# A graph-layer kernel's edge sort: four-record chunks, batches of 28 columns in two groups, the last bucket's true end, and one logit moved

## The chip, the cores and the metric

The kernel runs on one core of one Trainium2 chip. The metric is device time in microseconds; lower is better. Names of engines: PE is TensorE, DVE is VectorE, ACT is ScalarE, POOL is GpSimd, SP is SyncE, which only issues transfers and waits.

## What is computed

```python
xn = _layernorm(x)                                   # x: 6250 nodes x 256
x = x + gnn(xn, edge_weight, edge_weight_n2, ..., src, dst) + mix(xn)
x = x + ffn(_layernorm(x))                           # the best half of the nodes, by a score
...
# gnn: 106250 edges
low  = relu(segment_sum(val_low[:, None]  * (xn @ weight_low)[col],  row))    # row = src, col = dst
high = relu(segment_sum(val_high[:, None] * (xn @ weight_high)[col], row))
mlp  = relu(xn @ weight_mlp)
logits = concat([low @ att_low, high @ att_high, mlp @ att_mlp])
att = softmax(sigmoid(logits) @ att_vec / 3)
out = 3 * (att[:, 0:1] * low + att[:, 1:2] * high + att[:, 2:3] * mlp)
```

`mix` is an attention with one 32 x 32 matrix per head, summed over all nodes, and a GELU layer behind it.

## The kernel before, in words

The edges come unordered by `src`. The kernel sorts them into 98 buckets of 64 nodes, and then sums each bucket with matmuls.

**The sort.** The edges lie on 128 partitions. A batch is BB = 30 columns of them (3840 edges), and there are G = 28 batches. A batch is split into GROUPS = 3 groups of GS = 10 columns. For each batch DVE builds one-hots (`one_hot`, L733), sums them (`sum_hots`, L746 to L752), PE adds them up into ranks (`ranks`), ACT copies the ranks (`copy_rank`, L1313), DVE picks each edge's rank (`pick_rank`, L766) and makes its place (`place`, L777 to L793). ACT turns the places into one-hots, group by group (`quotients`: one activation per column, L1303, then one ReLU over the group, L1307), DVE multiplies records with cells (`cell_records`, L811), and PE permutes the batch with one matmul per column (`permute`). `stage_records` (L1322) copies the result; `destinations` (L827, L829) makes the indices; POOL scatters it to `sorted_records` in DRAM (`scatter`, L648) with UNITS = 16 indirect DMAs, each of which writes for 128 partitions one chunk of two records (32 bytes). Each batch's share of a bucket is padded to a whole number of chunks.

**What goes on beside it.** `schedule` puts one batch in a slot, and gives the first 14 slots the layer norm (`ln_moments`, `ln_apply`) and the attention's K and V sums for 13 quads of node tiles, and the later slots the rest of `mix` (`hidden`, `mlp`, `mix_end`, `mix_out`). Slot 13 folds the weights. With SPILL = 2 the last two mixes run in slots after the last batch. `mix_out` also makes the third attention logit, a product and a sum over a quad (L895, L898, into `l3`). Each engine runs its list in the order that its `slot` writes. In a mix slot PE permutes groups 0 and 1 of the batch before, transposes the first pair of tiles (`turn(0)`, L1602), permutes group 2, transposes the second pair, and goes on to destinations, the mix and the next ranks. ACT begins a slot with the quotients of group 2 of the batch before, right behind `copy_rank`.

**The bucket loop.** SP loads the sorted records; PE and ACT turn them to columns of 128 records. POOL gathers, column by column, the 128 rows of `xn_rows` that a column's records name, into a ring of 32 columns (L665). SP counts what has landed (`g_ready`, in fours) and tells POOL which columns are free (`col_free`, L564). Two buckets are one tile of 128 nodes. For each bucket DVE makes the weighted one-hots (`select`, L1116 and L1122), PE multiplies them with ten columns from the bucket's first on (five, then five), and with one more in a loop for each column beyond ten (`extras`). ACT copies the sums (L1490 and L1443), then come the two weight matmuls, the attention, and the FFN for the tile, spread over three stages. `ptab` holds where each bucket begins. Its entries from 98 on are set to the table's end, `COLS * P - 1`, so the last bucket reaches to column 851.

**The tail** picks the best half of the nodes by a search over thresholds, and stores the result.

```python
COLS = 4 * -(-(E + NB * G) // (4 * P))                          # 852 columns
for u in range(UNITS):                                          # scatter, L646
    pool.indirect_dma_start(rec_dram, ..., stage_rec[0:PR, par, u * 8:(u + 1) * 8], None)
for j in range(GS):                                             # quotients, L1302
    ins = act.activation(quot[:, j, :], iota32[:, :], ACT.Abs, ...)
act.activation(flat, flat, ACT.Relu, bias=ones_f[:, 0:1], scale=-1.0)
step(dve.memset(pclip[:, NB:NR], float(COLS * P - 1)))          # the last bucket's end
```

## Time and profile before

| | us |
|---|---|
| median of 3 timed runs | 1985.35 (1983.74 to 1985.68) |
| profiled execution, first to last instruction | 2481.7 |
| its time as a run of its own | not recorded beside the span |
| busy in it: PE, DVE, ACT, POOL | 1719.4, 1229.1, 924.8, 1371.7 |

The profiled execution is 496 us longer than the timed ones. Its span is told in microseconds from the first instruction. The sort runs from 63 us (the first scatter) to 813 us, the bucket loop from 832 to 2405 us, the tail to 2481.7 us. A matmul of PE in fp32 leaves two records; ends of matmuls are modelled. "issue" marks idle time for which the profile shows no wait.

### The profile page before, as it was taken

The numbers are of one execution on the slowest core, as the hardware profiler recorded it, in microseconds if no ns is written. First come the engines' busy times: TensorE is split into PE (matmuls) and PEld (weight loads), VectorE is DVE, ScalarE is ACT, GpSimd is POOL, SyncE is SP. The second block draws the span as 40 slices with busy tenths as digits, with TensorE's granted clock in tenths as the row PEclk, the third lists the DMA queues.
The fourth block names the chain that finished last, engine by engine and source line by source line (L and its number), as shares of the span: only waits on it lengthen the run. The fifth ranks groups of instructions, "written<-read, shape, count | busy, mean of one in ns | idle before, by whom it ended". The sixth has DMA issues, their size and how long they took to land.

```text
span 2481.7 us, 30518 instructions
## 1 busy us (share of the span) xinstructions
PE 1719.4 (69%) x9109; PEld 1441.9 (58%) x9109; DVE 1229.1 (50%) x3164; ACT 924.8 (37%) x2641; POOL 1371.7 (55%) x1351
## 2 busy tenths in 40 slices
PE   4788884998865347776777677677577677667672
PEld 4566673887754335665665666566466566556562
DVE  8899995888761223432343333333333333333336
ACT  2677873777652112321222222222222222222223
POOL 3277675788776565545555455455455545554600
PEclk9899996999967667888887888788788788788886
DMA  3221211111100422222222222222222222222303
GB/s 90 72 63 54 80 33 30 46 54 46 46 5 5 133 85 72 78 69 75 71 74 71 68 73 75 65 72 75 68 73 75 75 69 71 81 71 68 85 9 104
DMA packets 102212, 162.99 MB, mean 66 GB/s; under 512 B 32190, under 2 KB 72762, under 8 KB 102040
## 3 DMA queue, kind: packets, MB, share of 16 engines
q0 software_dynamic: 55232, 113.59, 16.4%
q1 hardware_dynamic: 46808, 47.29, 6.0%
q8 instruction: 85, 1.39, 0.2%
q14 instruction: 87, 0.71, 0.1%
HBM read 139.76 MB, written 21.04 MB: 65 GB/s over the span
## 4 chain that ended last, share of the span: by engine, by line
PE 51%; issue 23%; DVE 10%; ACT 9%; another core or an unknown queue 5%; DMA 1%; SPq 1%; POOL 0%; DVEq 0%; ACTq 0%; POOLq 0%
PE bank L1528 49%; ACT side L1303 2%; PE bank L1817 1%; ACT base L1303 1%; ACT arena L1303 1%; DVE arena L811 1%; ACT arena L1447 1%; ACT arena L1443 1%; DVE arena L733 1%; ACT side L1519 1%; DVE arena L766 1%; ACT arena L1307 0%; PE bank L1602 0%; DVE arena L781 0%
## 5 line engine op out<-in xcount | busy, mean ns | idle before, releaser
L1528 PE MATMUL bank<-arena 128*128 128x128 f32 (+3 forms) x6320 | 1292.5, 359 | 508.2 <-issue 426.8
L1528 PEld LDWEIGHTS bank<-arena 128*128 128x128 f32 (+1 forms) x6320 | 1094.8, 205 | 683.8 <-issue 500.0
L665 POOL DMA_INDIRECT arena<-xn_rows,arena x852 | 825.5, 969 | 733.8 <-SPq L564 450.0
L648 POOL DMA_INDIRECT sorted_records<-arena x448 | 523.0, 1167 | 256.0 <-issue 139.3
L1167 DVE CUSTOM_DVE_ANT_0 arena<-arena 128x256 f32<-128x256 f32 x98 | 37.8, 423 | 414.9 <-ACT arena L1452 376.1
L1122 DVE TENSOR_TENSOR arena<-arena 128x640 f32<-128x640 bf16 (+1 forms) x204 | 164.2, 805 | 47.6 <-DVE arena L1116 17.7
L1172 DVE SCALAR_TENSOR_TENSOR att_prod<-sg,att_neg 128x9 f32<-128x9 f32 x49 | 8.5, 174 | 334.9 <-issue 300.8
L1490 ACT ACTIVATE arena<-bank 128x256 f32<-128x256 f32 x49 | 18.8, 383 | 355.5 <-remote 262.1
L1116 DVE SCALAR_TENSOR_TENSOR arena<-io,arena 128x320 bf16<-128x320 f32 (+1 forms) x204 | 97.8, 479 | 106.3 <-DVE wall L1209 43.5
L1528 PE MATMUL bank<-arena,base 128*128 128x128 f32 (+3 forms) x766 | 118.4, 287 | 16.7 <-ACT base L1307 8.3
L1438 ACT ACTIVATE arena<-bank,b1f 128x128 f32<-128x128 f32 x392 | 110.3, 372 | 33.5 <-PE bank L1528 28.1
L811 DVE TENSOR_TENSOR arena<-arena 128x1280 f32<-128x1280 bf16 x84 | 120.5, 1488 | 4.1 <-remote 1.7
L1528 PEld LDWEIGHTS bank<-arena,base 128*128 128x128 f32 (+2 forms) x766 | 110.2, 211 | 17.6 <-ACT base L1307 8.5
L1443 ACT ACTIVATE arena<-bank 128x256 f32<-128x256 f32 x49 | 18.8, 383 | 247.0 <-PE bank L1528 219.3
L1528 PE MATMUL bank<-side,arena 128*128 128x512 f32 x196 | 97.1, 619 | 0.3 <-issue 0.3
L1481 ACT ACTIVATE side<-bank,wall 128x256 f32<-128x256 f32 x49 | 23.1, 472 | 176.0 <-remote 165.3
L1303 ACT ACTIVATE base<-arena 128x128 f32<-128x128 f32 x280 | 84.7, 391 | 9.4 <-DVE arena L792 9.4
L1468 ACT ACTIVATE nr<-nri 128x1 f32<-128x1 f32 x49 | 9.9, 203 | 206.0 <-issue 159.8
L1303 ACT ACTIVATE arena<-arena 128x128 f32<-128x128 f32 x280 | 84.6, 397 | 0.0
L1303 ACT ACTIVATE side<-arena 128x128 f32<-128x128 f32 x280 | 84.6, 392 | 0.0
L1528 PE MATMUL bank<-arena,side 128*128 128x128 f32 x560 | 73.5, 282 | 12.0 <-issue 10.9
L1528 PEld LDWEIGHTS bank<-arena,side 128*128 128x128 f32 x560 | 68.0, 196 | 15.6 <-issue 14.1
(312 smaller groups left out, 1889.2 us busy)
## 6 DMA issues: line engine op xcount, KB each, us to landing
arena<-xn_rows,arena POOLq DMA_INDIRECT x852
sorted_records<-arena POOLq DMA_INDIRECT x448
arena<-in_x SPq DMA_DIRECT2D x12, 512.0 KB
xn_rows<-arena SPq DMA_DIRECT2D x12, 512.0 KB
x_plus_xn_rows<-arena SPq DMA_DIRECT2D x12, 512.0 KB
arena<-x_plus_xn_rows SPq DMA_DIRECT2D x12, 512.0 KB
arena<-xn_rows SPq DMA_DIRECT2D x12, 512.0 KB
out<-base SPq DMA_DIRECT2D x4, 1024.0 KB
```

The lines of the kernel that those rows point to most:

```text
L648: pool.indirect_dma_start(rec_dram, bass.IndirectOffsetOnAxis(ap=idx[0:PR, par, u:u + 1], axis=0), stage_rec[0:PR, par, u * 8:(u + 1) * 8] ...
L665: pool.indirect_dma_start(gring[:, c % GR, :], None, xn_dram, bass.IndirectOffsetOnAxis(ap=rring[:, c, 3:4].bitcast(I32), axis=0)).then_in ...
L733: ins = dve.tensor_tensor(oh[:, t, :].rearrange("p j (h e) -> p j h e", e=2), twice[:, t, :].unsqueeze(2).to_broadcast([P, GS, NB // 2, 2] ...
L766: dve.tensor_tensor(prod4[:, :, :, 0:NB], oh[:, :, :].rearrange("p (s j) b -> p s j b", s=GROUPS), rankf[:, :].rearrange("p (s b) -> p s b ...
L811: dve.tensor_tensor(cellrec[:, t, :].rearrange("p t (f c) -> p t f c", f=4), cell[:, t, :].unsqueeze(2).to_broadcast([P, GS, 4, GC]), raw[ ...
L1116: return dve.scalar_tensor_tensor(out_, io64[:, :].unsqueeze(1).to_broadcast([P, n, BK]), float(BK * b), r[:, :, 0:1].to_broadcast([P, n, ...
L1122: return dve.tensor_tensor(out_, hots.unsqueeze(2).to_broadcast([P, n, 2, BK]), r[:, :, 1:3].unsqueeze(3).to_broadcast([P, n, 2, BK]), ALU ...
L1167: ins = dve.tensor_tensor_reduce(out=lg_prod[:, k, :], in0=lh[:, k * D:(k + 1) * D], in1=att_rows[:, k, :], scale=1.0, scalar=0.0, op0=ALU ...
L1303: ins = act.activation(quot[:, j, :], iota32[:, :], ACT.Abs, bias=p32[:, par, s * GS + j:s * GS + j + 1], scale=-1.0)
L1438: act.activation(fh[:, f, :], bank[4 + part][:, (f % 4) * P:(f % 4 + 1) * P], ACT.Gelu_apprx_tanh, bias=b1f[:, f:f + 1]).then_inc(S("fh_re ...
L1443: act.activation(agg[:, 1, :], bank[1][:, 0:D], ACT.Copy).then_inc(S("agg_b"), 1)
L1528: return pe.matmul(out_, lhsT, rhs, start=start, stop=stop, **kw)
```

## The change

A chunk holds REC = 4 records (64 bytes) instead of two, so a batch needs 8 scatters instead of 16, and each batch's share of a bucket is padded to a multiple of four. A batch is BB = 28 columns in two groups of 14, and there are G = 30. That makes COLS = 900 columns and eight blocks of records instead of seven. The last bucket ends where its records end. All 13 mixes fit in slots 14 to 26, and nothing spills. The third logit is made in the bucket loop, tile by tile, and `l3` is gone. The last tile's mask is made by DVE instead of POOL. The quotients of a batch are in two parts: group 0 in the batch's own slot, group 1 at the start of the next. Some tiles move.

```diff
-HG = 6
-BB = 30
-GS = 10
+HG = 7
+BB = 28
+GS = 14
+REC = 4
-    UNITS = GC // 2
+    UNITS = GC // REC
-    COLS = 4 * -(-(E + NB * G) // (4 * P))
+    COLS = 4 * -(-(E + (REC - 1) * NB * G) // (4 * P))
-    SPILL = 2
+    SPILL = 0
...
             def load_mix(a, par):
-                wait(sp, S("l3_ready"), a - 1)
+                wait(sp, S("mix_read"), a - 1)
...
                     pool.indirect_dma_start(
                         rec_dram, bass.IndirectOffsetOnAxis(ap=idx[0:PR, par, u:u + 1], axis=0),
-                        stage_rec[0:PR, par, u * 8:(u + 1) * 8], None).then_inc(S(f"scattered{par}"), 16)
+                        stage_rec[0:PR, par, u * 4 * REC:(u + 1) * 4 * REC], None).then_inc(S(f"scattered{par}"), 16)
...
-            pool.wait_ge(S("w_ready"), T)
-            pool.affine_select(out=wkey[:, T - 1:T], in_=wall[:, T - 1:T], compare_op=ALU.is_ge, fill=SENTINEL,
-                               base=TAIL - 1, pattern=[[0, 1]], channel_multiplier=-1).then_inc(S("w_masked"), 1)
...
                     dve.tensor_tensor(many[:, :, :, :], h[:, :, 0:H], h[:, :, H:GS], ALU.add).then_inc(S("many_set"), 1)
                     dve.wait_ge(S("many_set"), 4 * g + 1)
+                    dve.tensor_tensor(many[:, :, 0:3], many[:, :, 0:3], many[:, :, 4:7], ALU.add).then_inc(S("many_set"), 1)
+                    dve.wait_ge(S("many_set"), 4 * g + 2)
                     dve.tensor_tensor(many[:, :, 0:2], many[:, :, 0:2], many[:, :, 2:4], ALU.add).then_inc(S("many_set"), 1)
...
                 ins.then_inc(S("mix_read"), 1)
-                dve.wait_ge(S("mix_read"), a + 1)
-                dve.wait_ge(S("mlp_ready"), 2 * a + len(pairs_of(a)))
-                dve.tensor_tensor(xl[:, par, 0:m, :], side[:, ds(FOUR * a * D, m * D)].rearrange("p (t d) -> p t d", d=D),
-                                  att_mlp[:, :].unsqueeze(1).to_broadcast([P, m, D]), ALU.mult).then_inc(S("l3_prod"), 1)
-                dve.wait_ge(S("l3_prod"), a + 1)
-                dve.tensor_reduce(l3[:, ds(FOUR * a, m)], xl[:, par, 0:m, :], AX.X, ALU.add).then_inc(S("l3_ready"), 1)
...
-            step(dve.memset(pclip[:, NB:NR], float(COLS * P - 1)))
...
-                dve.tensor_copy(lg[:, 2:3], l3[:, ds(i, 1)])
+                    dve.wait_ge(S("mlp_ready"), 2 * NQ - 1)
+                dve.tensor_tensor_reduce(out=ybuf[:, :], in0=side[:, ds(i * D, D)], in1=att_mlp[:, :], scale=1.0,
+                                         scalar=0.0, op0=ALU.mult, op1=ALU.add, accum_out=lg[:, 2:3])
                 dve.wait_ge(S("lh_ready"), i + 1)
...
+            step(dve.memset(wkey[:, T - 1:T], SENTINEL))
...
-            step(dve.tensor_copy(wkey[:, 0:T - 1], wall[:, 0:T - 1]))
-            dve.wait_ge(S("w_masked"), 1)
+            step(dve.tensor_copy(wkey[:, 0:T - 1], wall[:, 0:T - 1]), False)
+            step(dve.tensor_copy(wkey[0:TAIL, T - 1:T], wall[0:TAIL, T - 1:T]))
...
                 if in_slot(g - 1):
-                    quotients(g - 1, 2, 1 - par)
+                    quotients(g - 1, 1, 1 - par)
...
-                if in_slot(g):
-                    quotients(g, 1, par)
...
                 if in_slot(g - 1):
                     permute(g - 1, 0, 1 - par)
-                    permute(g - 1, 1, 1 - par)
                 turn(0)
                 if in_slot(g - 1):
-                    permute(g - 1, 2, 1 - par)
+                    permute(g - 1, 1, 1 - par)
                 turn(1)
```

How the order moves, at two places. First ACT in one mix slot, from the rank copy on (L1313, after the change L1303); L1303 and L1307 are the quotients (after: L1293 and L1297), L1326 a copy of transposed tiles, L1322 the staging, L1365 the GELU, L1371 the ReLU. Before:

```order
L1313 ACTIVATE arena<-bank 128x294
L1303 ACTIVATE arena<-arena 128x128 x10
L1307 ACTIVATE arena<-arena,ones_f 128x1280
L1326 ACTIVATE arena<-bank 128x512
L1303 ACTIVATE base<-arena 128x128 x10
L1307 ACTIVATE base<-base,ones_f 128x1280
L1326 ACTIVATE arena<-bank 128x512
L1322 ACTIVATE arena<-bank 128x128
L1365 ACTIVATE arena<-bank,b1p 128x256 x2
```

And with the change:

```order
L1303 ACTIVATE arena<-bank 128x196
L1293 ACTIVATE arena<-arena 128x128 x14
L1297 ACTIVATE arena<-arena,ones_f 128x1792
L1316 ACTIVATE arena<-bank 128x512
L1293 ACTIVATE arena<-arena 128x128 x14
L1297 ACTIVATE arena<-arena,ones_f 128x1792
L1316 ACTIVATE arena<-bank 128x512
L1312 ACTIVATE arena<-bank 128x128
L1355 ACTIVATE arena<-bank,b1p 128x256 x2
```

The part that stood behind the GELU (ten activations and a ReLU into `side`) is gone, and the two that are left, ahead of the GELU, are longer by four activations and by 512 columns.

Then PE in one mix slot, from the rank matmuls to the destinations (L1528 is every matmul, after the change L1515; L1602, after L1589, the transposes). Before:

```order
L1528 MATMUL bank<-arena,ones_b 128x98
L1528 MATMUL bank<-arena,base 128x128
L1528 MATMUL bank<-arena,ident 128x32
L1528 MATMUL bank<-arena,base 128x128 x9
L1528 MATMUL bank<-arena,side 128x128 x10
L1602 MATMUL bank<-ident,arena 128x128 x4
L1528 MATMUL bank<-arena 128x128 x10
L1602 MATMUL bank<-ident,arena 128x128 x4
L1528 MATMUL bank<-arena 128x2 x16
```

And with the change:

```order
L1515 MATMUL bank<-arena,ones_b 128x98
L1515 MATMUL bank<-arena 128x128
L1515 MATMUL bank<-arena,ident 128x32
L1515 MATMUL bank<-arena 128x128 x13
L1589 MATMUL bank<-ident,arena 128x128 x4
L1515 MATMUL bank<-arena 128x128 x14
L1589 MATMUL bank<-ident,arena 128x128 x4
L1515 MATMUL bank<-arena 128x2 x8
```

Ahead of the first transposes stand 14 permuting matmuls instead of 20, behind them 14 instead of 10, and the destinations are 8 instead of 16. On POOL 448 scatters become 240, and 852 gathers 900.

## Rows read from the trace of the kernel before

**Rows 1.** The page: its first line.

```profile
span 2481.7 us, 30518 instructions
```

**Rows 2.** Waits: engine, line <- what it waited for: us in all, times, longest.

```profile
PE bank L1528 <- issue: 454.7, 347, 9.2
POOL arena L665 <- SPq L564: 450.0, 67, 13.1
```

**Rows 3.** Groups by line: engine, operation, shapes, count | busy us, mean ns | idle before.

```profile
L665 POOL DMA_INDIRECT arena<-xn_rows,arena x852 | 825.5, 969 | 733.8 <-SPq L564 450.0 <-issue 283.8
L648 POOL DMA_INDIRECT sorted_records<-arena x448 | 523.0, 1167 | 256.0 <-issue 139.3 <-DVE arena L829 87.3 <-ACT arena L1322 29.5
...
L1167 DVE CUSTOM_DVE_ANT_0 arena<-arena 128x256 f32<-128x256 f32 x98 | 37.8, 423 | 414.9 <-ACT arena L1452 376.1 <-issue 38.9
```

**Rows 4.** Timeline: start, length, operation [idle before]. POOL, batches 2 and 10.

```profile
148.29 1.43 POOL L648 DMA_INDIRECT sorted_records<-arena  x1 [1.03 <-DVE arena L829]
...
355.59 1.43 POOL L648 DMA_INDIRECT sorted_records<-arena  x1 [2.52 <-DVE arena L829]
```

**Rows 5.** Timeline, POOL: batches 12 and 27, the first gather.

```profile
422.98 0.95 POOL L648 DMA_INDIRECT sorted_records<-arena  x1 [21.55 <-DVE arena L829]
...
793.34 0.96 POOL L648 DMA_INDIRECT sorted_records<-arena  x1 [8.17 <-DVE arena L829]
...
831.68 0.97 POOL L665 DMA_INDIRECT arena<-xn_rows,arena  x1 [18.44 <-issue]
```

**Rows 6.** Timeline, PE and ACT in a mix slot: permutations, rank copy, quotients.

```profile
521.88 2.50 PE L1528 MATMUL bank<-arena 128*128 128x128 f32 x20 [1.10 <-ACT arena L1307]
...
537.43 0.45 PE L1528 MATMUL bank<-arena,base 128*128 128x128 f32 x2
...
539.95 2.40 PE L1528 MATMUL bank<-arena,side 128*128 128x128 f32 x20
...
544.62 2.50 PE L1528 MATMUL bank<-arena 128*128 128x128 f32 x20 [1.84 <-ACT arena L1307]
...
539.85 0.41 ACT L1313 ACTIVATE arena<-bank 128x294 f16<-128x294 f32 x1 [1.11 <-remote]
540.16 3.02 ACT L1303 ACTIVATE arena<-arena 128x128 f32<-128x128 f32 x10
543.21 1.36 ACT L1307 ACTIVATE arena<-arena,ones_f 128x1280 f32<-128x1280 f32 x1
```

**Rows 7.** Timeline in the bucket loop: a bucket's matmuls, and two gathers.

```profile
1499.61 4.92 PE L1528 MATMUL bank<-arena 128*128 x20
...
1510.96 0.95 POOL L665 DMA_INDIRECT arena<-xn_rows,arena  x1 [0.30 <-SPq L564]
...
1518.46 1.07 POOL L665 DMA_INDIRECT arena<-xn_rows,arena  x1 [0.30 <-issue]
```

**Rows 8.** Timeline, the last tile: bucket copies, the last bucket's matmuls, an extra column.

```profile
2366.85 0.38 ACT L1443 ACTIVATE arena<-bank 128x256 f32<-128x256 f32 x1 [4.83 <-PE bank L1528]
...
2383.02 2.85 PE L1528 MATMUL bank<-arena 128*128 x12 [1.00 <-DVE arena L1122]
...
2387.77 0.22 DVE L1116 SCALAR_TENSOR_TENSOR arena<-io,arena 128x64 f32<-128x64 f32 x1 [1.06 <-PE bank L1528]
2389.49 0.22 DVE L1116 SCALAR_TENSOR_TENSOR arena<-io,arena 128x64 f32<-128x64 f32 x1 [1.06 <-PE bank L1528]
...
2405.07 0.38 ACT L1443 ACTIVATE arena<-bank 128x256 f32<-128x256 f32 x1 [19.14 <-PE bank L1528]
```

**Rows 9.** Timeline, DVE: rank picks of batches 14, 26 and 27, and batch 26's indices.

```profile
428.80 1.69 DVE L766 TENSOR_TENSOR arena<-arena 128x2940 f16<-128x2940 bf16 x1 [0.16 <-issue]
...
722.76 1.69 DVE L766 TENSOR_TENSOR arena<-arena 128x2940 f16<-128x2940 bf16 x1 [4.46 <-issue]
...
739.81 1.69 DVE L766 TENSOR_TENSOR arena<-arena 128x2940 f16<-128x2940 bf16 x1 [1.04 <-ACT arena L1313]
752.52 0.17 DVE L829 TENSOR_TENSOR arena<-arena,bank 128x16 int32<-128x16 f32 x1
```

More of the change, by code:

```diff
@@ L168, in build @@
         stage_rec = r1.take([P, 2, GC * 4])
-        quots = [base[:, spare:T * D].rearrange("p (j q) -> p j q", q=P), side[:, spare:T * D].rearrange("p (j q) -> p j q", q=P),
-                 r1.take([P, GS, P])]
+        quots = [r1.take([P, GS, P]) for _ in range(GROUPS)]
         iota_q = r1.take([P, STEPS], U16)
@@ L187, in build @@
         bmean = r1.take([P, 2 * HEADS])
-        att_mlp = r1.take([P, D])
         st4 = r1.take([P, FOUR, 6])
@@ L283, in build @@
         ptab = lead_take("side", [1, NR], I32)
-        pcol = r1.take([1, NB + 1])
-        starts = r1.take([1, 2, NB])
-        span = r1.take([1, NB])
-        over = r1.take([1, NB])
-        over_sum = r1.take([1, NB])
-        words = r1.take([1, NB])
+        pcol = lead_take("side", [1, NB + 1])
+        starts = lead_take("side", [1, 2, NB])
+        span = lead_take("side", [1, NB])
+        over = lead_take("side", [1, NB])
+        over_sum = lead_take("side", [1, NB])
+        words = lead_take("side", [1, NB])
         far = r1.take([P, 2, NB])
@@ L531, in _ @@
             sp.wait_ge(S("mix_read"), NQ)
-            sp.wait_ge(S("l3_ready"), NQ)
             for t, name in ((wlow, "L0_gnn_weight_low"), (whigh, "L0_gnn_weight_high")):
@@ L541, in _ @@
                 sp.wait_ge(S(f"scattered{par}"), SCAT * (G // 2))
-            rows = rec_dram.rearrange("(c h) f -> c (h f)", h=P // 2)
+            rows = rec_dram.rearrange("(c h) f -> c (h f)", h=P // REC)
             for k in range(NBLK):
@@ L775, in place @@
                 Q1 = 28
-                with nc.allow_low_precision(reason="whole numbers below 2 ** 13, one of a bucket's and at most nine ties"):
+                with nc.allow_low_precision(reason="whole numbers below 2 ** 13, one of a bucket's and at most thirteen ties"):
                     dve.tensor_tensor(prod[:, :, 0:H], prod[:, :, 0:H], prod[:, :, H:2 * H], ALU.add).then_inc(S("prod_half"), 1)
@@ L1048, in _ @@
             step(dve.tensor_copy(cnt_i[0:NR, :], bank[6][0:NR, 0:G]))
-            step(dve.tensor_scalar(cnt_b[0:NR, :], cnt_i[0:NR, :], 1, None, ALU.bitwise_and))
-            dve.tensor_tensor(runs[0:NR, :], cnt_i[0:NR, :], cnt_b[0:NR, :], ALU.add).then_inc(S("runs_ready"), 1)
+            step(dve.tensor_scalar(cnt_i[0:NR, :], cnt_i[0:NR, :], REC - 1, None, ALU.add))
+            step(dve.tensor_scalar(cnt_b[0:NR, :], cnt_i[0:NR, :], REC - 1, None, ALU.bitwise_and))
+            dve.tensor_tensor(runs[0:NR, :], cnt_i[0:NR, :], cnt_b[0:NR, :], ALU.subtract).then_inc(S("runs_ready"), 1)
             dve.wait_ge(S("runs_ready"), 1)
@@ L1416, in _ @@
             quotients(0, 0, 0)
+            ln_sqrt(0)
             quotients(0, 1, 0)
-            ln_sqrt(0)
-            quotients(0, 2, 0)
             stage_records(0, 0)
```

34 lines of the change are left out of this document (15 added, 19 removed).

## The prediction

> **What bounds the kernel now.** I read the page's span first, then the table of waits, POOL's own timeline, one slot on PE and ACT, and the end of the bucket loop. The profiled execution spans 2481.7 us [rows 1], while the timed runs take 1985.35 us. The 496 us between them have a place: in the bucket loop POOL is held back by SP's `col_free` for 450.0 us, and PE stands 454.7 us between instructions without a recorded reason [rows 2]. So the profiled loop is held by a PE that crawls; the timed one cannot be, for 49 tiles x 10 us are just the 496 us missing. The timed time is checked by a sum from the same trace. First gather at 831.7, less the 8.2 us that POOL waited for the last scatter batch while PE crawled [rows 5], is 823.5. Then 852 gathers at 0.969 + 0.30 = 1.27 us each [rows 3, 7] are 1082 us. From the last bucket's copy (2405.1) to the end are 76.6 us [rows 8], and some 8 us lie between the last column and that copy. Together 1990 us, 0.2% over the median. There is hardly room for idle time of POOL: **the timed bucket loop is set by POOL's gathers**, one per column.
>
> The sort before it has two halves. In slots 1 to 12 (LN and KV) POOL waits 2 to 4 us for each batch's indices (L829): the ring of VectorE, ACT and PE sets the slot, (355.59 - 148.29)/8 = 25.9 us [rows 4]. From slot 13 on POOL is back to back: batch 12 starts at 422.98, batch 27 at 793.34, of which 8.17 were a wait [rows 5], so (793.34 - 8.17 - 422.98)/15 = **24.1 us a batch of 16 scatters**. The ring alone would need less: PE's third permutation starts at 521.88 and again at 544.62, 22.7 us [rows 6].
>
> **The change, part by part.**
>
> *Scatters.* 448 become 240 (8 x 30). POOL's share of a batch falls from 24.1 us to 8 x 1.47 = 12 us [rows 3], so POOL stops setting the second half and the ring takes over.
>
> *The ring in a mix slot.* After the rank matmuls ACT copies the ranks at 539.85, then makes the last quotients of the batch before: 3.02 + 1.36 us, and PE's third permutation starts at 544.62, 0.05 us after them, having stood 1.84 us [rows 6]. With two groups of 14 the quotients left for this place take 14 x 0.302 = 4.2 and a ReLU over 1792 instead of 1280 columns, 1.9: 6.1 us in place of 4.4. PE has less to do meanwhile: from 537.43 to 542.78 it runs two permutations and four transposes, 5.35 us. The first took 2.52 us with the offsets; with 14 matmuls it is 8 records of 0.12 (2.40/20) longer, 3.5 us, and with the transposes 4.0. So PE reaches its last permutation at 541.4 and the quotients are ready at 546.3: a wait of 4.9 us, 3.1 more. What goes from PE is small: two permutation matmuls (0.44), eight destination matmuls (0.2), a third of the rank columns (0.1). So 22.7 - 0.7 + 3.1 = 25.1 us at most. But ACT sees the ranks 2.4 us after PE has left them (537.43 to 539.85), so PE still has work in hand when it stands, and part of the wait is covered; were all of it covered, the slot would be 22.0. I take **23.6 us**, the middle, and keep 22.0 and 24.8 (part of the top goes into waits that PE has later in the slot anyway).
>
> *Length of the second half.* Before: pick 14 starts at 428.80 [rows 9], the last scatter ends at 813.24 (the first gather's start less its idle time, [rows 5]); less the wait of 7.9 above the usual 0.3, 376.6 us. Now slots 14 to 26 carry the thirteen mixes: 13 x 23.6 = 306.8. Two slots without a mix follow; one took 739.81 - 722.76 = 17.05 with three quotients of 4.4, now two of 6.1 and the same wait, 17.8: 35.6. From the last pick to its indices 752.52 - 722.76 = 29.8 [rows 9], then 8 scatters, 10. Together 382: **+6 us** (-15 at 22.0, +21 at 24.8). The two added batches thus eat what POOL's relief gives. The spill slots vanish, but they ran beside scatters already.
>
> *First half.* VectorE's list gets shorter by about 1 us a slot (2744 for 2940 elements in the one-hots and products, half the step mask, half the destinations), but ACT and PE have the longer tail described above. Per slot from -1.0 to +0.25, over 12 slots: I take **-5** (-12 to +3).
>
> *Third logit.* In the mix slots a product and a sum over 1024 columns leave VectorE, which is not the bound there. In the bucket loop one product with its sum, 0.42 us like L1167 [rows 3], takes the place of a copy, ahead of the wait for `lh`, where VectorE idles: nothing on its own path. It can touch POOL: the gather at 1518.46, beside a two-input product of VectorE, took 1.07 instead of 0.95 [rows 7]. 0.12 x 49 = 6 at most; I take **+3**. The Trainium skill (SBUF — State Buffer, the section on the two separate sides) says that a VectorE operation holding both ports keeps GpSimd from writing DMA descriptors altogether; by that rule a gather would lose the operation's whole length, and the sum would gain up to 17 us more. The row shows 0.12 us lost, not 0.4, so the trace does not bear the rule out at that size.
>
> *Columns.* Padding to four records makes more columns. I counted from the inputs' edges: bucket 97 used to need all 852; now its first column is 859 and ten are read, which the counter, in fours, grants when 872 have landed. The other 28 gathers run into the tail, where only the stores wait, some 60 us later. **20 x 1.27 = +25 us** on the chain (the 900 gathers in full would be +61).
>
> *True end.* Before, bucket 97 was stretched to the table's end and ran eight extra columns, one iteration each 1.72 us [rows 8] on VectorE and PE in turn; behind gathers of 1.27 they end 4 to 5 us late, and its last selection and visit come after. Now its last selection is ready before the columns: **-7** (0 to -15). Three other buckets get one extra column each, hidden under gathers.
>
> *Rest.* The mask on VectorE instead of POOL: -1. One more block of records to turn, 0.9 us beside the first gathers: 0. Moved tiles, the histogram in banks of 8: 0, hidden by loads. SP's wait on `mix_read` instead of `l3_ready` lets the next x quad start 2.5 us earlier; PE did not wait for it: 0, and if it did, a gain.
>
> Sum: 6 - 5 + 3 + 25 - 7 - 1 = **+21 us**, from the median **2007 us** (+1.1%). About 0.2% (4 us) can be told from no change.
>
> **The rivals.**
>
> *A, the other side: the loop is not gather-bound.* Then the added columns are free. The one tile in which PE did not crawl went from the copy at 2366.85 to the next odd bucket at 2383.02 [rows 8], and that bucket's 20 records are 4.9 us more [rows 7]: 21.1 us, against 17.4 x 1.27 = 22.1 us for a tile's gathers. From 22.1 us a tile on, the ring of PE, ACT and VectorE decides. Then the eight extras cost their full 13.8 us and three come back (5.2): -8.6, with +1 for the sort and -1 for the mask: 1977. Against it: the sum above closes without idle time of POOL.
>
> *B: the ring is shorter when not profiled.* If the 2.5 us between PE's ranks and ACT are an effect of the records, a mix slot could fall to some 20.5 us: 13 x 3.1 = 40 less, the first half at -12: 2007 - 47 = 1960. For it: the profile did slow PE elsewhere. Against: POOL's wait in the first half shows the same ring, and no crawl is seen there.
>
> *C: the wait is not covered at all.* 24.8 a slot, first half +3, the third logit at 6: 2007 + 15 + 8 + 3 = 2033.
>
> *D: the change does not do what it says.* Excluded: the order of instructions shows 240 scatters.
>
> **Chances.** Forecast 0.57 (1992 to 2022), C 0.15, A 0.14, B 0.11, and 0.03 for what falls near no change. The range 1970 to 2034 leaves out B and a little of C's far end. Faster by over 0.2%: A, B, 0.25. Within: 0.07, the edges of A and the forecast. Slower: 0.68.
>
> **What would show it.** In the changed profile: 240 scatters at 1.27 us with waits for L829's successor in both halves; a mix slot of 23 to 24 us with PE standing some 5 us ahead of its second permutation, for ACT's ReLU; the first gather within a few us of 831; 900 gathers still at 1.27 to 1.28 us; no run of eight extras at the end. Wrong: a first gather before 800 (B), or a time that falls though the columns grew (A). A kernel of the old form with more columns gathered would settle A by itself.

## The result, and the profile after

| | kernel before | changed kernel |
|---|---|---|
| median of 5 timed runs, us | 1983.78 (1982.85 to 1985.68) | 1968.93 (1965.44 to 1972.10) |
| profiled execution, span, us | 2481.7 | 1970.4 (its own time 1972.10) |

The ratio is 0.9921 (0.9909 to 0.9934): the change makes the kernel 0.8% faster. The forecast was 2007 us, 1.1% slower, in a range that began at 1970. It missed, and with the wrong sign.

The two profiles were not taken under the same condition, and most of what follows hangs on that. In the profile of before PE "crawls": it stands 454.7 us between instructions with nothing recorded that it waits for [rows 2]. In the changed kernel's profile such stands come to 3.7 us. The crawl is not the kernel's. The kernel before, run again in six sets of comparisons, took 1985 to 1986 us in two of them and 2463 to 2517 us in four, one and the same chip showing both, and every kernel that ran in those four shows the crawl. The timed runs above belong to the 1984 kind, the profile of before to the other.

The page of the changed kernel, its span, the engines, POOL and the clock by fortieths of the span:

```profile
span 1970.4 us, 29835 instructions
...
PE 1566.6 (80%) x8859; PEld 1335.3 (68%) x8859; DVE 1210.8 (61%) x3172; ACT 905.1 (46%) x2623; POOL 1182.1 (60%) x1190
...
POOL 4124444333334466777777777777777777777770
PEclk9899999799999976899999999999999999999995
```

Its groups, as in [rows 3]: 900 gathers, now 994 ns each where they were 969, 240 scatters, and POOL waiting 350.7 us for indices where it waited 87.3. SP's `col_free` is named for 19.2 us in all, 0.3 at most each time, not for 450.0:

```profile
L663 POOL DMA_INDIRECT arena<-xn_rows,arena x900 | 894.4, 994 | 280.3 <-issue 261.2 <-SPq L562 19.2
L646 POOL DMA_INDIRECT sorted_records<-arena x240 | 265.7, 1107 | 449.6 <-DVE arena L823 350.7 <-issue 67.8 <-ACT arena L1312 31.1
```

POOL's timeline, to be laid beside [rows 4, 5]: batches 2, 10, 14 and 25, the last scatter, the first gather and gather 871, the last that the loop needs; then ACT's copy of the last bucket:

```profile
146.13 0.96 POOL L646 DMA_INDIRECT sorted_records<-arena  x1 [12.14 <-DVE arena L823]
...
332.38 0.96 POOL L646 DMA_INDIRECT sorted_records<-arena  x1 [10.97 <-DVE arena L823]
...
426.98 0.96 POOL L646 DMA_INDIRECT sorted_records<-arena  x1 [11.68 <-DVE arena L823]
...
678.96 0.96 POOL L646 DMA_INDIRECT sorted_records<-arena  x1 [10.42 <-DVE arena L823]
...
748.20 0.96 POOL L646 DMA_INDIRECT sorted_records<-arena  x1 [0.30 <-issue]
755.61 0.97 POOL L663 DMA_INDIRECT arena<-xn_rows,arena  x1 [6.46 <-issue]
...
1886.54 0.96 POOL L663 DMA_INDIRECT arena<-xn_rows,arena  x1 [0.30 <-issue]
...
1891.98 0.38 ACT L1430 ACTIVATE arena<-bank 128x256 f32<-128x256 f32 x1 [2.49 <-PE bank L1515]
```

Read: KV slots of (332.38 - 146.13)/8 = 23.3 us; mix slots of (678.96 - 426.98)/11 = 22.9; a first gather at 755.6, 76 us ahead of that in [rows 5]; (1886.54 - 755.61)/871 = 1.298 us a gather, with POOL idle for its usual 0.30 only. So POOL waits for indices ahead of every batch of the sort, and in the loop it has no slack.

### The profile page after: what moved, and what is told of

It is laid out like the page before. It is cut to its first block, busy times and chain, and to the rows that moved or that the text cites. A ratio compares the mean times of both kernels' runs of the same rounds, so it can differ in the third digit from the quotient of the medians.

```text
span 1970.4 us, 29835 instructions
## 1 busy us (share of the span) xinstructions
PE 1566.6 (80%) x8859; PEld 1335.3 (68%) x8859; DVE 1210.8 (61%) x3172; ACT 905.1 (46%) x2623; POOL 1182.1 (60%) x1190
## 4 chain that ended last, share of the span: by engine, by line
POOL 34%; issue 14%; DMA 9%; SPq 2%; DVE 2%; ACT 1%; PE 1%; POOLq 0%; ACTq 0%; DVEq 0%
POOL arena L663 34%; DMA arena<-xn_rows,arena 9%; SPq L556 1%; ACT side L1506 1%; PE bank L1515 1%; DVE arena L1239 0%; DVE arena L1241 0%; POOL sorted_records L646 0%; SPq L561 0%; SPq L559 0%; DVE base L1281 0%; DVE arena L1238 0%; DVE arena L1246 0%; DVE kc L1244 0%; DVE kc L1245 0%
## 5 line engine op out<-in xcount | busy, mean ns | idle before, releaser
L1515 PE MATMUL bank<-arena 128*128 128x128 f32 (+2 forms) x7222 | 1311.6, 341 | 245.7 <-SPq L552 85.6
L1515 PEld LDWEIGHTS bank<-arena 128*128 128x128 f32 x7222 | 1137.3, 198 | 393.7 <-issue 174.8
L663 POOL DMA_INDIRECT arena<-xn_rows,arena x900 | 894.4, 994 | 280.3 <-issue 261.2
L646 POOL DMA_INDIRECT sorted_records<-arena x240 | 265.7, 1107 | 449.6 <-DVE arena L823 350.7
L1293 ACT ACTIVATE arena<-arena 128x128 f32<-128x128 f32 x840 | 251.3, 391 | 8.2 <-DVE arena L786 8.2
L1109 DVE TENSOR_TENSOR arena<-arena 128x640 f32<-128x640 bf16 x199 | 162.6, 817 | 28.8 <-DVE arena L1103 0.5
L1103 DVE SCALAR_TENSOR_TENSOR arena<-io,arena 128x320 bf16<-128x320 f32 x199 | 96.5, 485 | 82.3 <-issue 38.5
L805 DVE TENSOR_TENSOR arena<-arena 128x1792 f32<-128x1792 bf16 x60 | 118.9, 2022 | 2.3 <-PE bank L1515 1.3
L1297 ACT ACTIVATE arena<-arena,ones_f 128x1792 f32<-128x1792 f32 x60 | 107.3, 1789 | 1.9
L1515 PE MATMUL bank<-side,arena 128*128 128x512 f32 x196 | 94.0, 601 | 0.0
L1457 ACT ACTIVATE nr<-nr,const 128x1 f32<-128x1 f32 x147 | 56.8, 386 | 4.9
L1515 PEld LDWEIGHTS bank<-side,arena 128*128 128x128 f32 x196 | 37.7, 192 | 26.3 <-issue 24.8
L1515 PEld LDWEIGHTS bank<-base 128*128 128x128 f32 (+2 forms) x212 | 36.4, 200 | 27.7 <-issue 27.7
```

What stands on the lines that cost most here:

```text
L646: pool.indirect_dma_start(rec_dram, bass.IndirectOffsetOnAxis(ap=idx[0:PR, par, u:u + 1], axis=0), stage_rec[0:PR, par, u * 4 * REC:(u + 1 ...
L663: pool.indirect_dma_start(gring[:, c % GR, :], None, xn_dram, bass.IndirectOffsetOnAxis(ap=rring[:, c, 3:4].bitcast(I32), axis=0)).then_in ...
L805: dve.tensor_tensor(cellrec[:, t, :].rearrange("p t (f c) -> p t f c", f=4), cell[:, t, :].unsqueeze(2).to_broadcast([P, GS, 4, GC]), raw[ ...
L1103: return dve.scalar_tensor_tensor(out_, io64[:, :].unsqueeze(1).to_broadcast([P, n, BK]), float(BK * b), r[:, :, 0:1].to_broadcast([P, n, ...
L1109: return dve.tensor_tensor(out_, hots.unsqueeze(2).to_broadcast([P, n, 2, BK]), r[:, :, 1:3].unsqueeze(3).to_broadcast([P, n, 2, BK]), ALU ...
L1293: ins = act.activation(quot[:, j, :], iota32[:, :], ACT.Abs, bias=p32[:, par, s * GS + j:s * GS + j + 1], scale=-1.0)
```

## The experiments

Each ran beside the kernel before, on the same chip. Ratios are to that.

**1. A first set: the kernel before again, the true end alone, four-record chunks alone, the square root moved.** In this set PE crawled.

The kernel before, unchanged.

> The kernel before, unchanged, for a profile in which PE does not crawl. Time 1984. The changed kernel's profile has 1.298 us from gather to gather and 83 us from the last column the loop needs to the end. Theory 1: the loop of the kernel before has the same 1.30 a gather where PE does not crawl, so that the first gather must start near 1984 - 83 - 852 x 1.298 = 795, some 37 us earlier than in the profile of before (the sort was longer there too). Theory 2, the prediction's: 1.27 a gather and a first gather at 815 to 825. If PE crawls again (span over 2400) neither can be told.

2472 us, one run. PE crawls, so neither theory could be told; but it shows that the crawl also strikes in the sort. PE's timeline, in a KV slot:

```profile
326.64 0.39 PE L1528 MATMUL bank<-arena,base 128*128 128x128 f32 x2 [0.94 <-issue]
328.08 0.59 PE L1528 MATMUL bank<-arena,base 128*128 128x128 f32 x2 [1.05 <-issue]
330.19 0.37 PE L1528 MATMUL bank<-arena,base 128*128 128x128 f32 x1 [1.52 <-issue]
```

Permuting matmuls that take 0.12 us each elsewhere [rows 6] come one or two at a time, a microsecond apart. The burst lasts from 323 to 342 us, and POOL's next batch waits 22.1 us.

The true end alone:

```diff
-            step(dve.memset(pclip[:, NB:NR], float(COLS * P - 1)))
```

> The kernel before with the true end of the last bucket alone. 844 columns are needed instead of 852 and the eight extra columns go. Gather-bound loop (the prediction): 8 x 1.28 = 10 us less for the columns and 0 to 15 for the extras, about 15 in all, 0.8%. Loop bound by the ring of PE, ACT and VectorE (rival A): 8 x 1.72 = 14. If the last columns were hidden: 0 to 3.

0.9955 (0.9928 to 0.9982), 11 us. In a crawling loop, in which POOL waits for SP, this says nothing of gathers.

Chunks of four records with the true end, still 28 batches in three groups of ten (884 columns are gathered):

```diff
-    UNITS = GC // 2
-    CAP = 2 * STEPS
-    COLS = 4 * -(-(E + NB * G) // (4 * P))
+    UNITS = GC // REC
+    CAP = REC * STEPS
+    COLS = 884
...
-                        stage_rec[0:PR, par, u * 8:(u + 1) * 8], None).then_inc(S(f"scattered{par}"), 16)
+                        stage_rec[0:PR, par, u * 4 * REC:(u + 1) * 4 * REC], None).then_inc(S(f"scattered{par}"), 16)
...
-            step(dve.memset(pclip[:, NB:NR], float(COLS * P - 1)))
```

> The kernel before with chunks of four records alone (28 batches, three groups of ten, 8 scatters a batch) and the true end; 868 columns needed, 884 gathered. Prediction's pricing: mix slots fall from POOL's 24.1 to the ring's 22.7 and the slots after them more, about -25 in the second half, -12 at most in the first, +16 x 1.30 = +21 for columns, -7 for the end: near -15. Rival, the relief of POOL is worth nothing because ACT and PE hold the slot at 24: +14. Rival, POOL's relief also shortens the first half's slots from 25.9 to the 23.4 of the changed kernel: -40.

0.9598 (0.9566 to 0.9630), 2365 us where the kernel before takes 2463: a gain of 98 us, more than any of the three had it. The first gather is at 717.9 instead of 833.4. Mix slots are 19.9 us. The prediction had said that the ring alone needs 22.7.

ACT's square root ahead of the quotients of group 1:

```diff
-                if in_slot(g):
-                    quotients(g, 1, par)
                 if ln is not None:
                     ln_sqrt(ln)
+                if in_slot(g):
+                    quotients(g, 1, par)
```

> The kernel before with ACT's square root of the layer norm ahead of the quotients of group 1 instead of behind them. Theory: in the first twelve slots VectorE stands 1.7 us a slot for that square root (13.8 us in eight slots of the profile of before), and the changed kernel loses the wait because those quotients are gone from there. Then the slot falls from 25.9 to POOL's 24.1 or a bit more: -12 to -20 us. Rival: the wait only moves to the quotients' reader (PE's permutation) and the slot stays at 25.9: 0.

1.0091 (1.0056 to 1.0127), slower. VectorE's waits for the root are gone, and two others stand in their place. Waits of DVE and of PE, 150 to 360 us:

```profile
DVE arena L863 <- ACT base L1355: 19.6, 8, 2.5
```

```profile
PE bank L1528 <- ACT arena L1307: 25.4, 8, 3.2
```

The slot is 26.8 us. This theory of mine fell. VectorE's wait at L848 for that root, on which it rested, is itself seen in crawling executions only: 14.4 us in eight waits from 150 to 360 us of the profile of before, 1.5 us in one wait of this set's kernel before, and none in the profile of experiment 3.

**2. A second set: the changed kernel, four-record chunks alone, the third logit, twice the scatters.** The kernel before took 1984.8 us here.

The changed kernel, unchanged.

> The changed kernel, unchanged. In the runs just made the kernel before took 2463 us, with PE standing some 430 us in the bucket loop for nothing that is recorded, where it took 1984 in the comparison with the change. Theory: that is a property of the chip or its state, not of the kernel. Where the kernel before takes 1984 this takes 1969; where it takes 2463 this has the same crawl and gains only what its sort is shorter (first gather 756 against 833), less a longer loop: 2390 to 2420. Rival: the crawl hangs on the code, and the change removes it: 1970 on a chip where the kernel before takes 2463.

1969.18 us, 0.9922 (0.9909 to 0.9935), the first result again.

> Chunks of four records and the true end alone, in three groups of ten and 28 batches, once more, beside the changed kernel on the same chip. Its first gather was at 718 us, against 756 in the changed kernel and 833 in the kernel before, since its mix slots take 19.9 us against 22.9. Theory: the two groups of 14 and the two added batches of the change cost 38 us, so this is 30 to 45 us faster than the changed kernel: 1925 to 1940 where that takes 1969, 2365 where the kernel before takes 2463. Rival: the loop takes it back (its third logit copy, 868 columns against 872, nothing else differs there): same as the changed kernel.

**1923.22 us, 0.9694 (0.9681 to 0.9707).** It is 46 us faster than the changed kernel, of which the first gather explains 45 (708.9 against 753.9 in the run beside it). So much does the rest of the change cost in sum: the two larger groups, the two added batches, the third logit moved and the spill gone. Experiment 3 takes out one part of it. The mix slot on PE, as in [rows 6], with no gap between two rows (windows 524 to 565 of the first set's trace):

```profile
524.74 2.25 PE L1529 MATMUL bank<-arena,base 128*128 128x128 f32 x18
526.83 2.40 PE L1529 MATMUL bank<-arena,side 128*128 128x128 f32 x20
529.06 0.60 PE L1603 MATMUL bank<-ident,arena 128*128 128x128 f32 x4
529.50 2.40 PE L1529 MATMUL bank<-arena 128*128 128x128 f32 x20
...
544.65 2.25 PE L1529 MATMUL bank<-arena,base 128*128 128x128 f32 x18
```

Third logit out (a copy of one column in its place, so that logit is not computed):

```diff
-                dve.tensor_tensor_reduce(out=ybuf[:, :], in0=side[:, ds(i * D, D)], in1=att_mlp[:, :], scale=1.0,
-                                         scalar=0.0, op0=ALU.mult, op1=ALU.add, accum_out=lg[:, 2:3])
+                dve.tensor_copy(lg[:, 2:3], att_mlp[:, 0:1])
```

> The changed kernel without the third logit's product and sum in the bucket loop: a copy of one column takes its place (that logit is left out of the computation). Prediction: the product slows gathers beside it by 0.12 us, 49 times at most, so this is 3 us faster (0 to 6). Rival by the Trainium skill's rule on the two sides (SBUF — State Buffer), a gather loses the whole 0.4 us: 17 to 20 us faster. Where PE crawls in the loop: 0.

1969.66 us against 1969.18, each to some 3 us. The traces are finer: from the first gather to gather 871 it takes 1130.9 us without the product, and 1129.8 and 1130.9 in the two profiles with it; the gathers take 993 ns without it, 992 and 994 with it. So the 3 us of the prediction are not there. Nor are the 17 more that it drew from the Trainium skill (SBUF — State Buffer, the section on the two separate sides). What that section says of descriptors that GpSimd cannot write, it says of VectorE's 2-port modes; of an operation with two inputs it says only that it contends with a GpSimd operation that reads SBUF. Whether a gather, which reads its indices from SBUF, counts as one, it leaves open. The prediction applied the first to the second; this run shows no block for this product.

Eight more scatters a batch into a table that nobody reads:

```diff
+                for u in range(UNITS):
+                    pool.indirect_dma_start(
+                        rec2_dram, bass.IndirectOffsetOnAxis(ap=idx[0:PR, par, u:u + 1], axis=0),
+                        stage_rec[0:PR, par, u * 4 * REC:(u + 1) * 4 * REC], None).then_inc(S(f"scattered{par}"), 16)
```

> The changed kernel with eight more scatters of the same records a batch, into a second table that nobody reads: POOL's work in the sort as in the kernel before, all else as changed. Theory: POOL then sets the slot again, 24.2 us in place of 22.9 in mix slots and of 13.7 to 17 in the last four, and 24.2 in place of 23.3 in the first twelve: 12 x 0.9 + 12 x 1.3 + 4 x 9 = about +60 us. Prediction's view (the ring is nearly as long as POOL's batch): +10 to +40.

2043.41 us, 1.0292 (1.0276 to 1.0309): 74 us more than the changed kernel, where the theory had 60 and the prediction's view 10 to 40. The first gather is at 828.2, again 74 us later. POOL is back to back from batch 1 on, 23.8 us a batch. So 16 scatters a batch instead of 8 cost the changed kernel 74 us, and with them it is 59 us slower than the kernel before. (They are 480 scatters in 30 batches, where the kernel before has 448.)

**3. A third set: a profile of the kernel before without the crawl, and ACT's part split.** The kernel before took 1985.7 us.

> The kernel before, unchanged, once more, for its profile on a chip where PE does not crawl. The changed kernel and the one with four-record chunks alone both gather at 1.30 us a column and end 82 to 89 us after the last column that is needed. Theory 1: so does this one, then its first gather is at 1983 - 90 - 851 x 1.30 = 787 and the sort is 40 us shorter than in the profile of before. Theory 2, the prediction's: first gather at 815 to 830 and 1.27 a column. Theory 3: first gather at 815 to 830, 1.30 a column, and an end much shorter than 90, or a time nearer 2015 when profiled.

1983.05 us, span 1981.3, no crawl. POOL: batches 2, 10, 14 and 26, the last scatter, the first gather and gather 851; then ACT's copy of the last bucket:

```profile
148.46 1.43 POOL L648 DMA_INDIRECT sorted_records<-arena  x1 [1.03 <-DVE arena L829]
...
342.05 1.05 POOL L648 DMA_INDIRECT sorted_records<-arena  x1 [0.30 <-issue]
...
441.65 1.43 POOL L648 DMA_INDIRECT sorted_records<-arena  x1 [1.65 <-DVE arena L829]
...
731.63 0.96 POOL L648 DMA_INDIRECT sorted_records<-arena  x1 [0.30 <-issue]
...
771.43 0.96 POOL L648 DMA_INDIRECT sorted_records<-arena  x1 [0.30 <-issue]
778.73 0.97 POOL L665 DMA_INDIRECT arena<-xn_rows,arena  x1 [6.33 <-issue]
...
1885.60 0.95 POOL L665 DMA_INDIRECT arena<-xn_rows,arena  x1 [0.30 <-issue]
...
1903.06 0.38 ACT L1443 ACTIVATE arena<-bank 128x256 f32<-128x256 f32 x1 [19.14 <-PE bank L1528]
```

Theory 1 holds, with a first gather still 8 us earlier than it said. KV slots are 24.2 us, not 25.9, which fits the 14.4 us that VectorE waited for the square root in the profile of before and does not wait here; the waits of 21.55 and 8.17 us in [rows 5] are 3.2 and 0.3 here, and the 18.44 ahead of the first gather are 6.33. The gathers come at 1106.9/851 = 1.30 us, where the profile of before gave 1.27. VectorE and PE ran less often beside them there; that this is why is not shown.

One mix slot of it, on ACT and PE. POOL's batch holds the ring by way of the staging buffer: ACT may not overwrite it before the scatters of two batches earlier have landed (37.3 us in seven waits from 430 to 670 us), the GELU stands behind that, and PE behind the GELU:

```profile
515.39 0.58 ACT L1326 ACTIVATE arena<-bank 128x512 f32<-128x512 f32 x1
520.21 0.28 ACT L1322 ACTIVATE arena<-bank 128x128 f32<-128x128 f32 x1 [4.24 <-DMA sorted_records<-arena]
520.38 0.83 ACT L1365 ACTIVATE arena<-bank,b1p 128x256 f32<-128x256 f32 x2
```

```profile
513.04 5.83 PE L1528 MATMUL bank<-arena 99*128 99x2 bf16 x40
521.36 0.27 PE L1528 MATMUL bank<-arena,ones_b 65*128 65x256 bf16 x1 [2.49 <-ACT arena L1365]
```

The true end alone, once more.

> The kernel before with the true end of the last bucket alone, once more, beside it on the same chip. Prediction's terms: eight gathers fewer in the wait, 10 us, and 7 for the extras (0 to 15): -17, between -10 and -25. Rival, the extras were hidden: -10. Where PE crawls it was -11 (0.9955, 0.9928 to 0.9982).

1962.01 us, 0.9886 (0.9871 to 0.9901), -23.7 us. The spans differ by 21.0 (1981.3 to 1960.3). In its trace gather 843, the last needed, starts at 1875.4 and the last bucket's copy is 7.9 us later; in the kernel before that distance is 1903.06 - 1885.60 = 17.5. So about 11 us are the eight gathers (1106.9 to 1095.8 us for the stretch) and 10 the extras.

The first seven activations of group 1 moved to the end of the batch's own slot:

```diff
-                    quotients(g - 1, 1, 1 - par)
+                    quotients(g - 1, 1, 1 - par, GS // 2, GS)
...
+                if in_slot(g):
+                    quotients(g, 1, par, 0, GS // 2)
                 if more:
                     copy_rank(g + 1)
```

> The changed kernel with the first seven activations of group 1's quotients made at the end of the batch's own slot, so that ACT begins the next slot with seven and the ReLU. Theory: in a mix slot PE stands 2.5 us for that ReLU, and the slot is 22.9 where it is 19.9 with three groups of ten. With 2.1 us taken from ACT's part the wait falls to 0.4 and the slot to 20.5 to 21: 12 x 2 = 24 us faster, 1945 where the changed kernel takes 1969. Rival: VectorE or the longer ReLU on ACT holds the slot, and the wait moves: 0 to -8.

**1933.98 us, 0.9750 (0.9725 to 0.9775)**, 35 us less than the changed kernel, and mix slots of 19.8 us. More than the 24 of the theory, and the clock accounts for the rest. Waits of PE from 480 to 620 us, in the changed kernel and in this one:

```profile
PE bank L1515 <- ACT arena L1297: 14.9, 6, 2.5
```

```profile
PE bank L1519 <- ACT arena L1299: 3.8, 7, 0.5
```

PE's last permutation in two neighbouring slots of the changed kernel, and after the short wait of this one (bracket: how long PE stood):

```profile
555.66 5.02 PE L1515 MATMUL bank<-arena 128*128 128x128 f32 x28 [2.47 <-ACT arena L1297]
...
579.02 3.39 PE L1515 MATMUL bank<-arena 128*128 128x128 f32 x28 [2.48 <-ACT arena L1297]
```

```profile
554.04 3.39 PE L1519 MATMUL bank<-arena 128*128 128x128 f32 x28 [0.54 <-ACT arena L1299]
```

And the windows of exactly the two in the changed kernel (last columns: busy times, then the granted clock, DMA share, GB/s):

```profile
555.66:560.68 5.02, 5.02 (x30) 5.02 (x31) 4.81 (x12) 4.99 (x16) 0.00 (x0) 0.66 0.34 108
...
579.02:582.41 3.39, 3.39 (x30) 3.39 (x31) 3.29 (x8) 3.39 (x12) 0.00 (x0) 1.00 0.59 150
```

After standing 2.5 us PE was granted 0.66 on average in the first, that is the lower level, 1.2 GHz, for two thirds of it (a mean of 0.66 between 1.0 and 0.5), and the full 2.4 GHz in the other. In that stretch the cost was 1.6 us. POOL's batches show the same: eight of the eleven mix slots between batches 14 and 25 are 23.3 or 23.4 us, and three are 21.7, so the clock costs 1.2 us a slot on average. After the ten stands of 0.54 us between 430 and 620 us of the split kernel all ten permutations took 3.39 us. Twelve mix slots of 2.0 us less stand and 1.2 us less clock are 38 us; the first gather came 36 us earlier (719.3 for 755.6).

A version with what had paid: four-record chunks in three groups of ten, the true end, the third logit in the bucket loop, and SP's loads of sorted records ahead of those of weights.

```diff
-                wait(sp, S("l3_ready"), a - 1)
+                wait(sp, S("mix_read"), a - 1)
...
             for k in range(NBLK):
                 n = min(P, READ - k * P)
                 sp.dma_start(rec_rows[0:n, k, :], rows[k * P:k * P + n, :]).then_inc(S("rec_loaded" if k else "rec_first"), 16)
+            for t, name in ((wlow, "L0_gnn_weight_low"), (whigh, "L0_gnn_weight_high")):
...
```

> Chunks of four records in three groups of ten and 28 batches, the true end, the third logit in the bucket loop, and SP's loads of the sorted records ahead of its five loads of weights. That kernel without the last two took 1923. Theory: the third logit costs nothing in the loop; in the last spilled mix it takes 0.9 us off what SP waits for, and the weights 2.5 us: 1920, 3 to 4 us less. Rival: the late weights hold up the first tile: 1923 or more.

**1906.82 us, 0.9613 (0.9599 to 0.9628)**, the fastest of all, 62 us under the changed kernel. 16 us less than without the last two, where 3 to 4 were expected: the first gather is at 692.8 instead of 708.9. Half of it is in the slots (the last batch starts 8 us earlier), half behind the last scatter; the two edits were not run apart. There, without them, the spilled mixes end after the last scatter and SP issues five loads of weights first. (Of what the changed kernel has besides chunks and true end, this version has the third logit's move. So the regrouping, with its two batches and without a spill, costs 46 to 62 us, an estimate from 1923, 1907 and 1969.) The stretch without the two edits:

```profile
691.13 0.96 POOL L649 DMA_INDIRECT sorted_records<-arena  x1 [0.30 <-issue]
708.85 0.97 POOL L666 DMA_INDIRECT arena<-xn_rows,arena  x1 [16.77 <-issue]
```

```profile
697.03 0.39 SPq L535 DMA_DIRECT2D arena<-in_L_gnn_weight_low  x1
...
699.49 5.02 SPq L547 DMA_DIRECT2D arena<-sorted_records  x7
```

**4. Further sets: gathers alone.** Twenty columns' rows fetched twice, and the 28 gathers of padding left out:

```diff
+                if c % 40 == 16 and c < 800:
+                    pool.indirect_dma_start(
+                        gring[:, (c + 7) % GR, :], None, xn_dram,
+                        bass.IndirectOffsetOnAxis(ap=rring[:, c + 7, 3:4].bitcast(I32), axis=0)).then_inc(S("again"), 16)
+                if c % 40 == 23 and c < 800:
+                    pool.wait_ge(S("again"), 16 * (c // 40 + 1))
```

```diff
-    QUADS = COLS // 4
+    QUADS = 872 // 4
...
-            for c in range(COLS):
+            for c in range(872):
```

> The changed kernel with 20 gathers more on POOL's path in the bucket loop: every fortieth column's rows are fetched twice, into the same place of the ring, seven columns ahead. Prediction's term: a gather that the loop must wait for costs its 1.27 to 1.30 us in full: +26 us, 1995 where the changed kernel takes 1969. Rival A: the loop has room, +0 to +8.

> The changed kernel with the gathers stopped at column 872, the last that the loop needs; the other 28 held only padding. Prediction: they run into the tail beside other work: 0 (-2 to +1). Rival: they hold back the last tile's loads or the stores of the result: -5 to -15.

> The changed kernel with 20 gathers more on POOL's path, once more (where PE crawled, the kernel before took 2510 and this 2483, which says nothing of POOL's path). Where the kernel before takes 1984: +26 us, 1995, if the loop is bound by the gathers; 1969 to 1977 if it has room.

> The changed kernel without the 28 gathers of padding, once more. Where the kernel before takes 1984: 1969 (-2 to +1) if they were hidden in the tail, 1955 to 1964 if they held back the last tile or the stores. Where PE crawls it took 0.969 of the time of before.

> As before, the changed kernel with 20 gathers more on POOL's path. Where the kernel before takes 1984: 1995 if the loop is bound by the gathers, 1969 to 1977 if it has room. Where it takes 2460: 0.998 of it, as in the run before.

> As before, the changed kernel without the 28 gathers of padding. Where the kernel before takes 1984: 1969 if they were hidden, 1955 to 1964 if not. Where it takes 2460: 0.975 of it.

All three sets fell into the crawl: the kernel before took 2510, 2464 and 2517 us, the one with more gathers 0.9923, 0.9985 and 0.9950 of it, the one with fewer 0.9694, 0.9749 and 0.9654. So these two near copies of the changed kernel crawl as well (PE stands 403 to 489 us with nothing recorded), and the crawl does not hang on the old code. Of a loop bound by gathers they say nothing, since POOL waits for SP there (386 us in the second of them with more gathers). That the kernel with 48 gathers fewer is still 57 to 67 us faster under the crawl I did not foresee. The traces place it: the gather of column 871 starts 28 to 45 us earlier, counted from the first gather, and the end comes 111 to 113 us after it, where it comes 129 to 130 us after it in the kernel with more gathers. So under the crawl the 28 gathers of padding are not free. Why both cost so much stays open.

## Why the prediction was wrong

Both spans cut at the same places, without the crawl:

| us | before (set 3) | changed | difference | predicted |
|---|---|---|---|---|
| to the first gather | 778.7 | 755.6 | -23.1 | 0 (second half +6, first -5, mask -1) |
| to the last needed gather | 1106.9 | 1130.9 | +24.0 | +25, and third logit +3 |
| from there to the end | 95.7 | 83.9 | -11.8 | -7 |
| sum | 1981.3 | 1970.4 | -10.9 | +21 |

(The medians differ by 14.9; this profiled execution of the changed kernel is the slowest of its five.)

- **What bounds the loop: right.** POOL's gathers, 0.30 us apart in both. The 20 added columns were predicted at 25 us, and the table has 24 for the stretch. The run meant to show it fell into the crawl, but four kernels without the crawl agree: 844, 852, 868 and 872 needed columns take 1095.8, 1106.9, 1127.7 and 1130.9 us, 1.30 each, with POOL's waits above its usual 0.30 at 2 us or less in all. The padding's zero was not tested alone without the crawl; with 8, 16 and 28 gathers of it behind the last needed one, the end comes 84.9, 84.6 and 83.9 us after that one, so no cost of 20 more is seen there.
- **The check of the timed time: wrong, and it closed.** It gave 1990 for 1985 from three parts that were each off: the first gather 45 us too late (823.5 for 778.7), the gathers 25 us too short (1082 for 1107), the end 11 too short (84.6 for 95.7). A sum that closes within 0.2% looked like proof that only the loop was disturbed in the profile. The sort was too.
- **"The ring alone would need less: 22.7 us": the step that failed first.** The ring alone needs 19.9. In experiment 2, with POOL out of the way, PE is busy without a gap: 140.00 of 140.00 us (row below, of the 1923 us run: window, its length, then the busy times of PE, its weight loads, DVE, ACT and POOL). The kernel before does it too where POOL does not hold it: in experiment 3's profile the third permutation starts at 470.48, 490.43 and 510.37 (second fence).

```profile
480.00:620.00 140.00, 140.00 (x954) 124.95 (x953) 132.91 (x211) 120.75 (x305) 72.49 (x57) 1.00 0.19 57
```

```profile
470.48 2.40 PE L1528 MATMUL bank<-arena 128*128 128x128 f32 x20
...
490.43 2.40 PE L1528 MATMUL bank<-arena 128*128 128x128 f32 x20
...
510.37 2.40 PE L1528 MATMUL bank<-arena 128*128 128x128 f32 x20
```

The 22.7 us were a reading of the disturbed profile. Between 521.88 and 544.62 PE stands 0.56 us for a GELU and 1.84 us for the ReLU, and the second stand goes back to the 2.3 us from PE's last rank matmuls to ACT's copy at 539.85 [rows 6]. In experiment 3's profile ACT's copy starts 0.04 us after the same matmuls, in all eleven slots from 420 to 660 us, and PE never stands for that ReLU. The matmuls in the profile of before, then matmuls and copy in experiment 3's:

```profile
537.30 0.29 PE L1528 MATMUL bank<-arena,ones_b 128*128 128x196 bf16 x2
```

```profile
505.05 0.29 PE L1528 MATMUL bank<-arena,ones_b 128*128 128x196 bf16 x2
505.38 0.42 ACT L1313 ACTIVATE arena<-bank 128x294 f16<-128x294 f32 x1 [0.78 <-PE bank L1528]
```

So POOL's relief was worth 24.2 - 19.9 = 4.3 us a mix slot, not 1.4. What delays ACT in the profile of before stays open, as the crawl does.
- **The longer tail of ACT: right in place, its size met by luck.** The term was 3.1 us a slot, a stand that grows from 1.84 to 4.9 us, of which the forecast took half. The stand was 0 with three groups and 2.5 us with two. Experiment 3 takes 2.0 us of it away and gets 3.1 (22.9 to 19.8), the rest being the clock, which the prediction had not counted. The changed kernel's 22.9 lies in the range 22.0 to 24.8, since two errors met in it: a base 2.8 us too long, and a tail charged at half of its 3.1 us.
- **"Length of the second half", +6: it was -12.** From the rank pick of batch 14 to the end of the last scatter 382 us were predicted for the changed kernel and 359.7 were measured. Twelve slots at 22.8 instead of 23.6 are -9.5. The thirteenth mix was charged like the others, and it has one tile (49 = 12 x 4 + 1): 16.2 for 23.6, -7.4. The two slots without a mix and the end are -5.7. Of that, 3.5 us are a slip in the sum: 17.05 us less three quotients of 4.4 and plus two of 6.1 are 16.1 for such a slot, not 17.8; 17.4 and 15.8 were measured. Before the change the same stretch took 372.1, not 376.6. The picks after the change, on DVE:

```profile
389.48 1.59 DVE L760 TENSOR_TENSOR arena<-arena 128x2744 f16<-128x2744 bf16 x1
...
663.25 1.59 DVE L760 TENSOR_TENSOR arena<-arena 128x2744 f16<-128x2744 bf16 x1 [5.54 <-ACT arena L1303]
679.41 1.59 DVE L760 TENSOR_TENSOR arena<-arena 128x2744 f16<-128x2744 bf16 x1
696.83 1.59 DVE L760 TENSOR_TENSOR arena<-arena 128x2744 f16<-128x2744 bf16 x1 [1.97 <-ACT arena L1303]
```

- **First half, -5: it was -11,** inside its -12 to +3 (that pick moved from 400.30 to 389.48). Without the crawl VectorE is the busiest engine in the KV slots of the kernel before, 174.1 of 180 us from 150 to 330, and the slot is 24.2. With its shorter list the slot is 23.3; no run takes that list apart.
- **True end, -7: -12 in the change,** inside 0 to -15. The eight extras cost 10 in the kernel before, by experiment 3's run of the true end alone.
- **Third logit, +3: 0**, by its own run. The 0.12 us that one gather took longer beside a product [rows 7] was no price for this one.
- **Rivals.** A, the loop not bound by gathers, is out by the traces without a crawl. B named the place: the 2.5 us between PE's ranks and ACT, and a first gather well ahead of 831. It took them for an effect of recording, which they are not, since experiment 3's profile is recorded too and has 0.04 us there. It had 0.11 and should have had most of what the forecast had; its 1960 is 9 us too low, since it has the mix slot at 20.5 us, and ACT's longer tail and the clock make it 22.9.

## What to carry over

Before a duration is taken from a profile whose span isn't the timed time, look for the disturbance in every stage, not only where it is largest; a closing sum of disturbed parts proves nothing. The period of a ring says what it needs only where nothing else adds to it: follow each waiting engine one step further (here PE to ACT, and ACT to its late start or to landed scatters), and count the bounding engine's work in a slot. Fewer and larger groups lengthen the part that comes last in a ring: four-record chunks with the true end gave 3.1%, of which the true end alone gives 1.1%, and what came with them, the regrouping above all, took back three quarters of the 3.1%.

## What the runs showed of the hardware

- The same kernel on the same chip took 1985 and 2517 us in different sets; in the second case PE issues single matmuls 1 to 3 us apart with nothing recorded between, in the sort too. Such stands come to 454.7 us in the profile of before and to 24.2 us in the same kernel's profile without the crawl. The cause stays open.
- After stands of 2.5 us PE ran its next 28 records at a granted 0.66 in one slot and at 1.00 in the next (5.02 against 3.39 us), and in 3.39 us after each of ten stands of 0.54 us.
- A product of VectorE with a sum over 256 columns, 49 times beside gathers, did not change their mean (992 and 994 ns with it, 993 without). In the kernel before, gathers take 994 ns without the crawl and 969 with it.
